# Transposed activations of a fused layer: half of the PSUM evictions moved from ScalarE to VectorE

## The reference

```python
def _layernorm(x, eps=1e-5):
    return (x - mean) / sqrt(var + eps)
# block 1, applied to h = _layernorm(x)
xn = (h - mu) * rsqrt(var + 1e-5) * gamma + beta
z, gate = split(xn @ W_in.T)              # 2 x 4096 columns
out = (z * sigmoid(clip(z))) * softmax(-dt) * silu(clip(gate))
x = x + (out @ W_out.T + h)
# block 2, applied to _layernorm(x): uint8 weights, 5632 hidden
x = x + down(silu(gate(hn)) * up(hn))
```

## Time and profile before

| what | us |
|---|---|
| runs without a profile | 7761.15 and 8732.41, median 8246.78 |
| the profiled execution | 7700.4 |
| its slowest core's span (core 5) | 7698.8 |
| spans of the 8 cores | 7643.1 to 7698.8 |
| TensorE busy in it | 6720.9 |
| the 128 evictions of line 730 | 99.9 |
| the 64 final adds of line 688 that read xres | 44.0 |

### The profile page before, as it was taken

How to read it: one execution, slowest core, us unless ns; L and a number is a source line. 1 busy time by engine, 2 the same in 40 slices (tenths; PEclk the granted TensorE clock), 3 DMA queues, 4 the chain that set the end, 5 groups by cost and what they waited for, 6 DMA issues and landing times.

```text
span 7698.8 us, 83890 instructions; the slowest of 8 cores (7643.1 to 7698.8 us)
## 1 busy us (share of the span) xinstructions
PE 6720.9 (87%) x30208; PEld 2974.9 (39%) x30208; DVE 1910.0 (25%) x3342; ACT 1237.6 (16%) x1572; POOL 339.2 (4%) x630
## 2 busy tenths in 40 slices
PE   3557676898999989999999989999899989999898
PEld 1223222343444434443444434444344434444343
DVE  3332322142112321142121421133111521123110
ACT  2111443111111121021211111011201111011110
POOL 1110222000000000000000000000000000000000
PEclk9778888998999989999999989999899989999999
DMA  5888455945457544856357454755458454665447
GB/s 173 276 268 268 161 203 195 299 167 202 142 205 238 178 167 153 273 170 224 121 185 258 157 188 153 249 192 201 142 159 287 149 196 152 216 204 185 162 153 246
DMA packets 386403, 1523.96 MB, mean 198 GB/s; under 512 B 31712, under 2 KB 31808, under 8 KB 369488
## 3 DMA queue, kind: packets, MB, share of 16 engines
q1 hardware_dynamic: 313488, 1195.46, 46.5%
q0 software_dynamic: 72512, 323.14, 12.7%
HBM read 1365.37 MB, written 153.11 MB: 197 GB/s over the span
## 4 chain that ended last, share of the span: by engine, by line
PE 76%; DMA 12%; DVE 5%; ACT 3%; issue 3%; POOL 0%; DVEq 0%; ACTq 0%; POOLq 0%; SPq 0%
PE pb L441 76%; DMA wgu_s<-wbt 3%; DMA win_s<-wbt 2%; DMA wd_s<-qo 1%; ACT xnT L730 1%; DVE bnb L593 1%; DMA qi<-woutT 1%; DMA out<-gsc 1%; DMA xb<-woutT 1%; DMA wout_s<-qo 1%; DMA qi<-winT 1%; DVE xres L649 1%; DVE gsc L688 0%; ACT qo L714 0%; ACT xn L770 0%
## 5 line engine op out<-in xcount | busy, mean ns | idle before, releaser
L441 PE MATMUL pb<-xnT,wbt 128*128 128x512 bf16 x16032 | 3638.5, 390 | 428.2 <-DVE wbt L575 258.6
L441 PEld LDWEIGHTS pb<-xnT,wbt 128*128 128x128 bf16 x16032 | 1596.3, 100 | 2450.5 <-issue 666.2
L441 PE MATMUL pb<-wbt,actb 128*128 128x512 bf16 x8032 | 1822.0, 386 | 156.5 <-DVE gsc L688 54.1
L441 PEld LDWEIGHTS pb<-wbt,actb 128*128 128x128 bf16 x8032 | 794.8, 99 | 1165.7 <-issue 259.7
L671 DVE SCALAR_TENSOR_TENSOR actb<-pb,suct,gsc 128x512 bf16<-128x512 f32 x352 | 264.4, 751 | 2030.4 <-PE pb L441 2025.5
L441 PE MATMUL pb<-xnT,qo 128*128 128x512 bf16 x3424 | 762.3, 381 | 3.7 <-ACT xnT L730 2.7
L784 ACT ACTIVATE gsc<-pb,sgct 128x512 f32<-128x512 f32 x352 | 242.6, 689 | 1875.8 <-PE pb L441 1871.5
L441 PEld LDWEIGHTS pb<-xnT,qo 128*128 128x128 bf16 x3424 | 336.2, 98 | 412.2 <-issue 12.2
L441 PE MATMUL pb<-idmt,xn 128*128 128x128 bf16 x1024 | 167.5, 289 | 335.7 <-ACT xn L761 118.7
L441 PE MATMUL pb<-qo,actb 128*128 128x512 bf16 x1696 | 398.7, 387 | 35.7 <-DVE gsc L688 19.0
L740 ACT ACTIVATE gsc<-gsc 128x512 f32<-128x512 f32 x256 | 161.6, 631 | 1185.3 <-DVE gsc L632 1182.4
(11 more groups left out here) (93 smaller groups left out, 1618.7 us busy)
## 6 DMA issues: line engine op xcount, KB each, us to landing
wbt<-wd_s SPq DMA_DIRECT2D x291, 1024.0 KB, 6.4
wbt<-wgu_s SPq DMA_DIRECT2D x246, 1024.0 KB, 5.2
wbt<-wout_s SPq DMA_DIRECT2D x211, 1024.0 KB, 6.3
wbt<-win_s SPq DMA_DIRECT2D x179, 1024.0 KB, 5.4
qo<-wgu_s SPq DMA_DIRECT2D x124, 512.0 KB, 4.0
qo<-wd_s SPq DMA_DIRECT2D x122, 512.0 KB, 6.1
qo<-win_s SPq DMA_DIRECT2D x90, 512.0 KB, 3.8
qo<-wout_s SPq DMA_DIRECT2D x90, 512.0 KB, 5.6
```

Source lines behind the costliest of these rows:

```text
L441: i = E.matmul(out_ap, lhsT, rhs, start=start, stop=stop) if E else None
```

## The change

The evictions of T1 are divided by parity. ACT keeps k = 0, 2, ..., 14 (bank pb[4]); DVE gets k = 1, 3, ..., 15 (bank pb[5]) as a tensor_scalar with multiply and add. In DVE's program they stand at the start of a pass: in pass 0 behind the first norm and the conversion of four weight slabs (items 0, 1, 3 and 4), in the other passes behind the eight final adds of the pass before. TensorE's waits before block k name the same evictions as before, which are now of two engines; ahead of the first product it waits for the evictions of block 14 and block 15.

```diff
@@ gen_tensor, after T1's loop over k @@
+                u.wait(E, f"T1ev:{p}:{ND - 2}")
                 u.wait(E, f"T1ev:{p}:{ND - 1}")
@@ gen_vector2, at the start of a pass @@
                     for i_ in (0, 1, 3, 4):
                         conv_op(i_)
+                for k in range(1, ND, 2):
+                    u.wait(E, f"T1mm:{p}:{k}")
+                    if p == 0 and k == 1:
+                        u.wait(E, "cst")
+                    op(lambda k=k: E.tensor_scalar(xnT[:, k * T:(k + 1) * T], pb[5][:, :],
+                                                   gcct[:, k:k + 1], bcct[:, k:k + 1], OP.mult, OP.add),
+                       f"T1ev:{p}:{k}")
                 for e in range(NZ):
@@ gen_scalar @@
-                for k in range(ND):
+                for k in range(0, ND, 2):
                     u.wait(E, f"T1mm:{p}:{k}")
                     if p == 0 and k == 0:
                         u.wait(E, "cst")
-                    op(lambda k=k: E.activation(xnT[:, k * T:(k + 1) * T], pb[4 + k % 2][:, :], AF.Identity,
+                    op(lambda k=k: E.activation(xnT[:, k * T:(k + 1) * T], pb[4][:, :], AF.Identity,
                                                 scale=gcct[:, k:k + 1], bias=bcct[:, k:k + 1]), f"T1ev:{p}:{k}")
```

## The result

The ratio of the changed kernel's time to that of before is 1.0069, 95% interval 1.0038 to 1.010: slower by some 53 us (0.0069 x 7700), well under 2%. The medians are 7813.68 us (20 runs) against 7761.15 us (19 runs); the profiled executions are 7746.64 and 7700.4 us.

A forecast was written before the change was run, and what follows sets the result against it. TensorE bounds the kernel (76% of the chain). Seven turns, 70.85 + 7 x 12.27 - 97.91 = 58.8 us, and pass 0's 0.35 give 59 us; on the base 7731 the forecast is 7790 us, range 7715 to 7870.

The forecast's parts named there:

- Rival (2): In T1: both engines evict side by side and T1 shrinks to half, 56 us less, 7675; chance 0.05.
- Rival (3): After T1: TensorE starts late but a later wait takes up the delay, no difference, 7731; chance 0.05.
- The base of the absolute number: Whole kernel: 7731 us, the middle of two single executions, to which the delay was added for 7790.
- The hold: At pass turns: block 1's eviction stands behind row block 3's adds on DVE; 8.3 us later at the turn examined.
- F: At each turn: time from ACT's first eviction to the end of row block 3's adds, 8.62 to 13.50 us.
- rival 1: At the turns: output stores land later still; delay 88 us, 7819 on the middle base; chance 0.08.
- The pace behind the adds: In T1 after the adds: DVE eviction 0.69 us, bank cycle 1.64, 12.27 us to the last eviction's end.
- 70.85: Seven turns from pass 1 on: sum in us of F, taken from the kernel before.
- pass 0: T1 there: DVE's conversion of item 4 stands ahead instead of adds; F = 1.96, delay 0.35 us.
- rival 4: First big matmuls: TensorE's clock stays at 0.50 for 5 us longer, 18 us more, 7808; chance 0.06.
- Two readers of PSUM: In T1: the skill's side-by-side reading alone promises half the length; the bank's round trip leaves 0.02 us per two blocks.

The follow-up runs named there:

- e1_interleaved: The change's division, but DVE's evictions of blocks 1 to 7 ahead of row block 3's final adds, later ones one behind each add; ratio to the kernel before 1.0003.
- e3_four_banks: The change's division, with DVE's evictions ahead of row block 3's adds and four banks instead of two; ratio to the kernel before 0.9975.

## Why the prediction was right, and where it was not

- **Direction and size of the difference.** A delay of 59 us was forecast on 7700.4, a ratio of 1.0077; measured is 1.0069 (1.0038 to 1.010). The mechanism was the one described: DVE's first eviction stands behind the adds, the adds behind the stores, and TensorE behind the eviction. Rival (2), a faster T1, did not come, since block 1 was held; and e1_interleaved shows that, with the hold mostly gone, two engines on two banks would have gained nothing either. Rival (3), a later wait that absorbs the delay, fell too, as TensorE's other waits stayed the same.
- **The base of the absolute number was the step that failed.** The working took 7731, midway between two single executions, and forecast 7790 us, while the median on show was 8246.78. Read against that, the number forecasts a fall of 5.5%, where the working forecasts a rise of 0.8% and a rise came. What the runs showed in place of 7731: the median of before is 7761.15 over 19 runs, 30 us higher, while the nine shortest lie between 7673.58 and 7704.69, some 40 lower; 7731 falls into the gap between the two, where no run lies. That 7790 came within 24 us of 7813.68, and inside the range, is partly luck, for that median is halfway between two runs of 7774.76 and 7852.60 with none between them. Only the difference was worked out; the base rested on two single executions.
- **The hold** was right. F was carried over from before, 8.6 to 13.5 us; after the change it is 7.4 to 13.5 in core 0. Over all eight cores the seven F sum to 69.1 us in the mean, against 68.7 before, so the stores did not land later (rival 1). DVE's first eviction starts 0.11 us behind the adds, for 0.10. That DVE's queue is first in, first out, as the Trainium skill says in "PSUM — Partial Sum Buffer", "Engine vs sequencer instructions", shows here as 9.27 us of TensorE waiting for an eviction whose input was long there.
- **The pace behind the adds** was mis-sized: DVE's eviction takes 0.81 us and not the 0.69 of the nearest row. Its bank's cycle is 0.14 + 0.77 + 0.81 = 1.72 us instead of 1.64. So the piece behind the adds is 22.67 - 9.71 = 12.96 us at the turn to pass 6 and 12.95 to 13.33 over the seven turns, instead of 12.27: 5.9 us more in all. ACT's 0.78, taken as the upper bound, was too low for it. Against that F was 2.3 us shorter in core 0 than the 70.85 assumed. By T1 the turns lose 160.3 - 97.9 = 62 us in core 0, against the 58.8 forecast; pass 0 lost 2.9 and not 0.35, since its conversion ended later (F = 3.81).
- **Whether the time rose by less than T1 says.** In the mean of the eight cores the seven turns lengthen from 97.7 to 161.0 us, by 63. The mean span rose by 54, but T1 of pass 1 also began 6 us earlier in that execution, so all but 3 us are accounted for. The 53 us of the ratio hang on few runs. It comes out as the mean of the ten shortest runs of the change, 7759.0, over that of the eleven shortest of before, 7706.1, and of these nine lie between 7673.58 and 7704.69 us and two at 7761.15 and 7778.91. Without those two the difference is 67 us, 0.87%. Their core spans are not on record, so nothing says whether the two belong there, and the loss is 53 to 67 us.
- **The clock** (rival 4) did not take part. At the turn to pass 6 the first big matmuls start at a granted clock of 0.50 and 5 us later it is 0.96; before, it was 0.50 in the first 5 us and 0.90 from 5945 to 5948:

```profile
5966.00:5977.00 11.00, 6.33 (x51) 4.52 (x49) 5.09 (x7) 4.68 (x6) 0.25 (x1) 0.50 0.40 139
5977.00:5982.00 5.00, 4.06 (x10) 1.46 (x11) 0.58 (x1) 0.00 (x0) 0.00 (x0) 0.50 0.00 0
5982.00:5985.00 3.00, 3.00 (x14) 1.30 (x13) 0.00 (x0) 0.00 (x0) 0.00 (x0) 0.96 0.00 0
```

- **Two readers of PSUM.** The Trainium skill, "PSUM — Partial Sum Buffer", "Specifications (TRN2)", says that ScalarE and VectorE read different banks side by side at full rate. The trace of e3_four_banks agrees: ACT's evictions take 0.78 and DVE's 0.81 us there beside each other, as they do apart. The rule was true and not enough; with two banks the round trip, 1.72 us for two blocks, set the pace.

## What to carry to other kernels

Before work is given to an idle engine, read what stands ahead of it in that engine's program and what that waits for: DVE was 25% busy and still the wrong place, since its queue was held by a store. An engine's rate and a buffer's round trip can be equal limits; here a second engine and more banks gained next to nothing alone, and together shortened T1 from 13.9 to 7.9 us. Forecast the difference first, and give the absolute time only as precisely as the base is known, on one stated base, so that it does not read as a change in the other direction.

## What was not expected of the hardware

A tensor_scalar on DVE that reads a PSUM bank of 512 f32, takes two per-partition scalars from SBUF and writes bf16 took 0.81 us (64 of them, 0.809 to 0.811), the one with two immediate constants and f32 output 0.69. The first multiplies and adds, the second takes a minimum and a maximum; which of these differences makes the 0.12 us was not tried. And an unsuspected stretch of the same kernel held nearly as much as the whole change cost: the store wait in the middle of each down product, worth some 46 us over 8 passes.
